# Softmax probabilities of the second attention transposed in ten blocks of 128 columns that cross head limits

## The chip, the cores and the metric

One core of one Trainium2 chip runs the whole program. The metric is the device time of one execution in microseconds (us); the time before is 1310.84 us, the median of three runs (1308.33 to 1314.42).

## The reference, cut to what matters

The program adds four residual blocks to `x` (2 x 1024 tokens x 256): an attention over 154 context tokens, a feed-forward block of eight experts (every token goes through all), a second attention with a mask over the same 154 context tokens, and a routed layer of eight experts. The change touches the second attention alone:

```python
q = xn @ Wq * scale                     # 8 heads of 64
kv = media @ Wkv                        # media: 2 batches x 154 tokens x 256
k, v = jnp.split(kv, 2, axis=-1)
q, k, v = (to_heads(q), to_heads(k), to_heads(v))
sim = jnp.einsum('bhid,bhjd->bhij', q, k)
sim = jnp.where(media_mask[:, None, None, :], sim, neg_inf)
attn = jax.nn.softmax(sim - max(sim), axis=-1)
out = jnp.einsum('bhij,bhjd->bhid', attn, v)
return out.transpose(0, 2, 1, 3).reshape(...) @ Wout
```

## The kernel before

The program has four stages in time: a first attention (0 to about 37 us of the span), the eight dense experts (to about 1046 us), the second attention with the routing of the third layer's tokens woven in (about 1046 to 1262 us), and the routed experts (to the end). Each engine's instruction order is written out by hand, and semaphores join the engines. TensorE (PE) runs its list in order, and so do VectorE (DVE), ScalarE (ACT), GpSimd (POOL) and SyncE (SP, which starts DMAs).

**Preparation of the second attention.** After the last expert product PE computes the keys (L1089) into banks 0 to 3, then the values (L1237): for each of the four halves of 77 context tokens (2 batches x 2 halves, `KH` = 77) two products with 512 moving columns, all heads at once. ACT copies each half into `V1` (L814; the trace calls it V). Then PE transposes the first chunk's normed tokens `xnC2` (L864; it waits for the last value copy and for `c_ln`, the end of DVE's second normalisation of the first chunk, L1327), ACT copies them (`xnT_out`, L749), and PE computes the queries (L1094).

**Chunks and tiles.** There are four chunks of 512 tokens, each of four tiles (j = 0 to 3) of 128 tokens. A tile goes like this:

- PE computes the scores of 8 heads x 154 keys in two halves of four heads (`scores`, L1109 and L1115).
- DVE takes the maxima (`maxes`, L1565), ACT the exponentials into `PC` (`exps`, L763, one instruction per head), DVE the reciprocals of the sums (`dens`, L1573), POOL multiplies by them (`normalise`, L538, a half of 616 columns at a time).
- PE transposes the probabilities (`p_transposes`, L1138). A head's 154 columns are cut in two halves of 77, so there are 16 transposes of 77 columns, in four groups of four. Groups 0 and 2 go to bank 0, which ACT copies to `PTC` (L769); groups 1 and 3 go to bank 1, which DVE copies (L1577). Group 2 waits for the copy of group 0, and group 3 for that of group 1.
- PE multiplies with the values (`attend`, L1148): per head two products, one for each half of 77 keys, 16 in all. Its group g waits for the copy of group g.
- DVE copies the result to `oT` (`o_out`, L1581), PE projects it (`project`, L1157), DVE adds it to the residual (`add_attention`, L1586).

A transpose is one PE record in the trace; an fp32 product is two (so `attend` shows x32). The order on PE in a chunk is: transposes of groups (0, 1) of tile j, `project` of tile j - 1, transposes of groups (2, 3), `attend` of tile j, scores of tile j + 2 or the like. Chunks 1 to 3 weave in the routing of the chunk before (`route`: `logits` L1169, `locations` L1176 to L1179, and on DVE `route_shift`, `route_choice`, `route_places`, `route_slots`; then POOL's `scatter`, L547). Chunks 0 to 2 prepare the next chunk (`front`): DVE's `front_variances`, `front_normed`, `front_variances2`, `front_normed2` (L1314, L1318, L1327, with POOL's power, L468), PE's transposes of `xnC2` and the next queries. After `add_attention` of tile 3 DVE's `route_normed` (L1327, rows) waits until the scatter before it has landed, and the last query copy (`q_out(f, 3)`, L1559) stands behind it.

**In the dense experts** POOL splits the weights (`split_hi`, `split_lo`); in `split_lo` it waits for `down_ps` and then writes `wd_hi` (L511) and `wd_lo` (L513).

## Time and profile before

| | |
|---|---|
| runs | 1308.33, 1310.84, 1314.42 us; median 1310.84 |
| profiled execution | 1310.67 us, of which the span from the first to the last instruction is 1308.9 us |
| busy share of the span | PE 96%, PEld 77%, DVE 70%, ACT 48%, POOL 40% |
| mean granted TensorE clock | 0.983 of full speed |
| second attention, preparation | 1046 to 1067 us |
| chunks 0, 1, 2, 3 from their first transposes of probabilities | 1073.8, 1116.5, 1168.6, 1215.2 us |

All times inside the execution are us from the start of the span. PE is the matrix engine's products, PEld its weight loads, which overlap them. The share of an engine is of busy time; it doesn't say that the others wait for it.

### The profile page before, as it was taken

To read this page: it belongs to the slowest core of one execution; us is meant where nothing else is said; L and a number is where in the kernel's file an instruction comes from. 1 tells how busy PE (TensorE), PEld (TensorE's weight loads), DVE (VectorE), ACT (ScalarE), POOL (GpSimd) and SP (SyncE) were. 2 spreads that over 40 slices of the span, in tenths; PEclk is the share of its full clock that TensorE was granted. 3 is DMA by queue.
4 is the path that set the end of the run, shared out by engine and by line. 5 is a ranking of instruction groups with operands and counts; after the bars stand their busy time and mean duration, and the time that the engine had idled before them with its cause. 6 is when DMAs were issued, how large, how long until landed. Compare 5 with 4: busy or idle time off the path is not lost.

```text
span 1308.9 us, 17566 instructions
## 1 busy us (share of the span) xinstructions
PE 1254.2 (96%) x6162; PEld 1008.3 (77%) x6162; DVE 914.7 (70%) x1643; ACT 624.4 (48%) x1320; POOL 530.1 (40%) x511
## 2 busy tenths in 40 slices
PE   7999999999999999999999999999999989989965
PEld 5778888888888888888888888888888747766754
DVE  5997777767777777777777677777776757757523
ACT  2465544555554555545455454545555343542521
POOL 3654644444444444444444444444442022333314
PEclk9999999999999999999999999999999999989978
DMA  4100500000010000000000001100001210011033
GB/s 132 49 1 1 178 25 25 25 25 25 30 44 25 25 25 25 25 25 25 25 25 26 25 25 41 33 25 25 25 1 49 65 49 17 1 49 49 17 108 128
DMA packets 44392, 50.34 MB, mean 38 GB/s; under 512 B 4289, under 2 KB 40182, under 8 KB 44175
## 3 DMA queue, kind: packets, MB, share of 16 engines
q1 hardware_dynamic: 40144, 43.03, 10.0%
q0 software_dynamic: 2048, 5.55, 1.2%
q8 instruction: 49, 0.80, 0.3%
q10 hardware_dynamic: 2111, 0.63, 0.2%
q14 instruction: 40, 0.33, 0.1%
HBM read 37.35 MB, written 12.62 MB: 38 GB/s over the span
## 4 chain that ended last, share of the span: by engine, by line
PE 87%; DVE 5%; ACT 2%; issue 2%; DMA 2%; POOL 1%; ACTq 0%; SPq 0%; another core or an unknown queue 0%; DVEq 0%; POOLq 0%
PE bank L959 25%; PE bank L958 25%; PE bank L960 25%; PE bank L1138 2%; PE bank L1157 1%; PE bank L1148 1%; ACT PC L763 1%; PE bank L1094 1%; PE bank L1285 1%; DMA slots<-rows,slot_c 1%; PE bank L1115 1%; PE bank L864 1%; DVE nmC L1565 1%; PE bank L1169 1%; PE bank L1237 1%
## 5 line engine op out<-in xcount | busy, mean ns | idle before, releaser
L958 PE MATMUL bank<-xop_hi,w_hi 128*128 128x512 f32 x896 | 350.9, 392 | 1.2 <-ACT half_g L696 1.2
L959 PE MATMUL bank<-xop_lo,w_hi 128*128 128x512 f32 x896 | 351.7, 393 | 0.0
L960 PE MATMUL bank<-xop_hi,w_lo 128*128 128x512 f32 x896 | 350.8, 392 | 0.0
L1505 DVE TENSOR_TENSOR acc<-bank,acc 128x512 f32<-128x512 f32 x248 | 170.8, 689 | 118.7 <-PE bank L960 118.4
L1491 DVE TENSOR_TENSOR hid_lo<-hid,hid_hi 128x512 fp32r<-128x512 f32 x256 | 214.8, 860 | 34.6 <-ACT hid_hi L719 34.5
L958 PE MATMUL bank<-hid_hi,wd_hi 128*128 128x512 f32 x512 | 202.5, 395 | 0.6 <-DVE hid_lo L1491 0.6
L959 PE MATMUL bank<-hid_lo,wd_hi 128*128 128x512 f32 x512 | 203.0, 396 | 0.0
L960 PE MATMUL bank<-hid_hi,wd_lo 128*128 128x512 f32 x512 | 201.4, 393 | 0.0
L958 PEld LDWEIGHTS bank<-xop_hi,w_hi 128*128 128x128 f32 x896 | 168.2, 188 | 42.2 <-ACT half_g L696 1.5
L959 PEld LDWEIGHTS bank<-xop_lo,w_hi 128*128 128x128 f32 x896 | 168.2, 188 | 38.2
L960 PEld LDWEIGHTS bank<-xop_hi,w_lo 128*128 128x128 f32 x896 | 168.1, 188 | 37.4
L704 ACT ACTIVATE s<-bank 128x512 f32<-128x512 f32 x128 | 78.2, 611 | 176.1 <-PE bank L960 176.1
L719 ACT CAST hid_hi<-hid 128x512 fp32r<-128x512 f32 x256 | 157.8, 624 | 1.9 <-DVE hid L1483 1.9
L680 ACT COPY bank<-bank 128x512 f32<-128x512 f32 x128 | 73.0, 570 | 123.7 <-PE bank L960 123.7
L483 POOL TENSOR_TENSOR w_raw<-raw_gu 128x256 f32<-128x256 f32 x32 | 24.1, 752 | 253.2 <-PE bank L960 253.2
L511 POOL CAST wd_hi<-raw_d 128x512 fp32r<-128x512 f32 x32 | 19.5, 611 | 242.3 <-PE bank L960 242.3
L960 PEld LDWEIGHTS bank<-hid_hi,wd_lo 128*128 128x128 f32 x512 | 96.4, 188 | 22.8
L958 PEld LDWEIGHTS bank<-hid_hi,wd_hi 128*128 128x128 f32 x512 | 96.1, 188 | 22.9 <-DVE hid_lo L1491 1.0
L959 PEld LDWEIGHTS bank<-hid_lo,wd_hi 128*128 128x128 f32 x512 | 96.0, 187 | 21.1
L1474 DVE TENSOR_TENSOR hid<-bank,s 128x512 f32<-128x512 f32 x128 | 87.8, 686 | 19.7 <-PE bank L960 19.7
L710 ACT ACTIVATE half_g<-half_g 128x512 f32<-128x512 f32 x128 | 81.2, 634 | 20.7 <-DVE half_g L1464 19.6
L503 POOL TENSOR_TENSOR w_lo<-w_raw,w_hi 128x1024 fp32r<-128x1024 f32 x32 | 86.6, 2707 | 4.0 <-DVE xnA L1327 1.6
(187 smaller groups left out, 1728.7 us busy)
## 6 DMA issues: line engine op xcount, KB each, us to landing
raw_gu<-in_L_ffn_Wg_dram SPq DMA_DIRECT2D x32, 256.0 KB, 2.7
raw_gu<-in_L_ffn_Wu_dram SPq DMA_DIRECT2D x32, 256.0 KB, 3.1
raw_d<-in_L_ffn_Wd_dram SPq DMA_DIRECT2D x32, 256.0 KB, 3.6
slots<-empty_row SPq DMA_DIRECT2D x1, 4112.0 KB, 15.3
kept<-slots SPq DMA_DIRECT2D x8, 258.0 KB, 4.3
x_res<-in_x_dram SPq DMA_DIRECT2D x4, 512.0 KB, 5.2
we_raw<-in_L_ffn_W_dram SPq DMA_DIRECT2D x8, 256.0 KB, 4.6
out_dram<-x_res SPq DMA_DIRECT2D x4, 512.0 KB
```

What stands on the lines that cost most here:

```text
L503: nc.gpsimd.tensor_tensor(out=lo[:, :, W_S1:W_S4 + 1], in0=s[:, :, W_S1:W_S4 + 1], in1=hi[:, :, W_S1:W_S4 + 1].bitcast(F32), op=ALU.subtract)
L680: nc.scalar.copy(bank[FORK_BANK[X]][:], bank[SUM_BANK[X]][:]).then_inc(forked[X], 1)
L704: nc.scalar.activation(out[:], ps[:], ACT.Silu).then_inc(silu_ready[h], 1)
L710: nc.scalar.activation(half["g"][:], half["g"][:], ACT.Silu).then_inc(silu_ready[h], 1)
L719: nc.scalar.copy(hid_hi[n % 2][h][:], hid[h][:]).then_inc(hi_ready[h], 1)
L958: mm(ps, w, a, start=start, stop=False, skip_group_check=True)
L959: mm(ps, w, a_low, start=False, stop=False, skip_group_check=True)
L960: return mm(ps, w_low, a, start=False, stop=True, skip_group_check=True)
L1138: ins = tr(bank[g % 2][0:KH, a * P:(a + 1) * P], PC[j % 2][:, n // 2, n % 2 * KH:(n % 2 + 1) * KH], ident[:])
L1474: nc.vector.tensor_tensor(out=hid[h][:], in0=ps[:], in1=s[:], op=ALU.mult).then_inc(hid_ready[h], 1)
L1491: nc.vector.tensor_tensor(out=hid_lo[n % 2][h][:], in0=hid[h][:], in1=hid_hi[n % 2][h][:].bitcast(F32), op=ALU.subtract).then_inc(lo_ready ...
L1505: nc.vector.tensor_tensor(out=to, in0=ps, in1=to, op=ALU.add).then_inc(acc_added, 1)
```

## The change

Eight heads of 154 columns lie side by side in `PC`, 1232 columns in all. They are now transposed in `PB` = 10 blocks of 128 columns (the last has 80), whatever head the columns belong to, in three groups: blocks 0 to 3 (bank 0, ACT copies 512 columns), 4 to 7 (bank 1, DVE copies 512 columns), 8 and 9 (bank 0, ACT copies 256 columns). Group 0 is issued where groups (0, 1) were, groups 1 and 2 where (2, 3) were. DVE has one copy of `PTC` per tile instead of two.

Seven of the ten blocks hold columns of two heads. `V1` now holds for each batch, block and up to two heads a 128 x 64 slice of the values, with zeros in the rows of the other head, so that `attend` is 17 products with 128 rows (the last block 80). To lay the values out so, ACT makes a copy `ctx2T` of the transposed context with the first 128 tokens appended, PE computes the values block by block (40 products of 128 or 64 moving columns instead of 8 of 512; the last group of the second batch after the transposes of `xnC2`), ACT copies six groups instead of four, and POOL multiplies them by a mask `vmask` (six instructions, `keep_own_heads`, behind the power of the second normalisation). `vmask` is made by 2 memsets and 14 selects on POOL in `split_lo` of the fifth weight quarter (`q == 4`). `attend` of a batch's first tile waits for `c_v`. The wait of the queries for `Wout` moves behind the transposes, and the bias load shares the semaphore `we_in`.

```diff
+    PW = HEADS * KEYS
+    PB = -(-PW // P)
+    P_BLOCKS = (range(0, 4), range(4, 8), range(8, PB))
+    V_BANKS = ((6, 7, 0), (1, 2, 7))
+    C_VALUES = 2 + HB // 2
...
+        PTC = sd.take("PTC", [P, PB, P], F32)
+        ctx2T = sd.take("ctx2T", [P, KB, B, KEYS + P], F32)
+        V1 = sd.take("V1", [P, B, PB, 2, HD], F32)
...
                 if q >= 2:
                     pool.wait_ge(down_ps, 4 * groups_through(q - 2))
+                if q == 4:
+                    v_masks()
                 nc.gpsimd.tensor_copy(wd_hi[i][:], d[:]).then_inc(wd_hi_ready, 1)
...
+            def keep_own_heads(b):
+                for g, of in enumerate(P_BLOCKS):
+                    pool.wait_ge(c_prep_act, C_VALUES + 3 * b + g + 1)
+                    v = V1[:, b, of[0]:of[-1] + 1, :, :].rearrange("p n s d -> p (n s) d")
+                    own = vmask[:, of[0]:of[-1] + 1, :].rearrange("p n s -> p (n s)")
+                    nc.gpsimd.tensor_tensor(out=v, in0=v, in1=own.unsqueeze(2).to_broadcast([P, 2 * len(of), HD]),
+                                            op=ALU.mult).then_inc(c_v, 1)
...
             power(LN_FRONT2, CT, 1)
+            pool.wait_ge(consts_ready, 3)
+            for b in range(B):
+                keep_own_heads(b)
             chunk(0, front=True, route=False)
...
+            act.wait_ge(p4_ps["u"], GROUPS)
+            ctx4 = ctxT[:].rearrange("p k (b n) -> p (k b) n", b=B)
+            wrapped = ctx2T[:].rearrange("p k b n -> p (k b) n")
+            nc.scalar.copy(wrapped[:, :, 0:KEYS], ctx4).then_inc(c_prep_act, 1)
+            nc.scalar.copy(wrapped[:, :, KEYS:KEYS + P], ctx4[:, :, 0:P]).then_inc(c_prep_act, 1)
...
-            for r in range(2 * B):
-                act.wait_ge(c_prep_ps, HB + r + 1)
-                nc.scalar.copy(V1[:, r, :], bank[V_PS[r]][0:KH, :]).then_inc(c_prep_act, 1)
+            for g in range(3):
+                value_out(0, g)
+            for g in range(2):
+                value_out(1, g)
             xnT_out(0)
+            value_out(1, 2)
             q_out(0)
...
             def p_transposes(c, j, groups):
-                pe.wait_ge(c_norm, 2 * t + groups[0] // 2 + 1)
+                pe.wait_ge(c_norm, 2 * t + (1 if groups == (0,) else 2))
+                flat = PC[j % 2][:].rearrange("p h k -> p (h k)")
                 for g in groups:
-                    if g >= 2:
-                        pe.wait_ge(c_pT_act if g % 2 == 0 else c_pT_dve, 2 * t + 1)
-                    for a in range(4):
-                        n = 4 * g + a
-                        ins = tr(bank[g % 2][0:KH, a * P:(a + 1) * P], PC[j % 2][:, n // 2, n % 2 * KH:(n % 2 + 1) * KH], ident[:])
+                    if g == 2:
+                        pe.wait_ge(c_pT_act, 2 * t + 1)
+                    for a, n in enumerate(P_BLOCKS[g]):
+                        w = block_rows(n)
+                        ins = tr(bank[g % 2][0:w, a * P:(a + 1) * P], flat[:, n * P:n * P + w], ident[:])
...
-                for g in range(4):
-                    pe.wait_ge(c_pT_act if g % 2 == 0 else c_pT_dve, 2 * t + 1 + g // 2)
-                    for h in (2 * g, 2 * g + 1):
-                        for k in range(2):
+                if t % (CB * CT) == 0:
+                    pe.wait_ge(c_v, 3 * b + 3)
+                for g, of in enumerate(P_BLOCKS):
+                    if g == 1:
+                        pe.wait_ge(c_pT_dve, t + 1)
+                    else:
+                        pe.wait_ge(c_pT_act, 2 * t + 1 + g // 2)
+                    for n in of:
+                        w = block_rows(n)
+                        for i, h in enumerate(block_heads(n)):
                             ins = mm(bank[5][h % 2 * HD:(h % 2 + 1) * HD, h // 2 * P:(h // 2 + 1) * P],
-                                     V1[:, 2 * b + k, h * HD:(h + 1) * HD], PTC[:, 2 * h + k, :], start=k == 0, stop=k == 1)
+                                     V1[0:w, b, n, i, :], PTC[0:w, n, :], start=n == head_blocks(h)[0], stop=n == head_blocks(h)[-1])
...
+            def values(b, g):
+                for a, n in enumerate(P_BLOCKS[g]):
+                    first, heads = n * P % KEYS, block_heads(n)
+                    cols = slice(INNER + heads[0] * HD, INNER + (heads[-1] + 1) * HD)
+                    for k in range(KB):
+                        ins = mm(bank[V_BANKS[b][g]][:, a * P:a * P + len(heads) * HD], ctx2T[:, k, b, first:first + P],
+                                 Wkvs[:, k, cols], start=k == 0, stop=k == KB - 1)
                 ins.then_inc(c_prep_ps, 1)
...
+            values(0, 0)
+            values(0, 1)
+            pe.wait_ge(c_prep_act, 3)
+            values(0, 2)
+            pe.wait_ge(c_prep_dve, 1)
+            values(1, 0)
+            pe.wait_ge(c_prep_act, 4)
+            values(1, 1)
+            pe.wait_ge(c_prep_act, C_VALUES + 4)
             pe.wait_ge(c_ln, 1)
             transpose_chunk(xnC2, (0, 1), 0, c_xnT_ps)
+            values(1, 2)
             pe.wait_ge(c_xnT, 2)
+            pe.wait_ge(c_prep_dve, HB // 2)
+            pe.wait_ge(wout_in, 16)
             queries(0)
...
                 maxes(c, 1, 1)
+                dens(c, 1, 0)
                 pT_out(c, 0, 1)
-                dens(c, 1, 0)
-                pT_out(c, 0, 3)
                 dens(c, 1, 1)
...
-                pT_out(c, 1, 1)
                 dens(c, 2, 0)
                 add_attention(c, 0)
-                pT_out(c, 1, 3)
+                pT_out(c, 1, 1)
...
-                pT_out(c, 3, 1)
                 if with_front:
                     front_variances2(f)
                 add_attention(c, 2)
-                pT_out(c, 3, 3)
+                pT_out(c, 3, 1)
```

## Rows read from the trace of the kernel before

**Rows 1.** Page: the chain that ended last, share of the span by engine.
```profile
PE 87%; DVE 5%; ACT 2%; issue 2%; DMA 2%; POOL 1%; ACTq 0%; SPq 0%; another core or an unknown queue 0%; DVEq 0%; POOLq 0%
```
**Rows 2.** Busy time by stretch: PE, PEld, DVE, ACT, POOL, then granted clock, DMA.
```profile
1067.00:1102.70 35.70, 32.68 (x321) 27.10 (x322) 26.26 (x70) 17.71 (x74) 11.84 (x10) 1.00 0.01 1
...
1160.00:1168.50 8.50, 7.68 (x46) 6.00 (x46) 4.35 (x13) 5.08 (x22) 2.43 (x2) 0.63 0.00 0
...
1237.00:1251.50 14.50, 13.54 (x105) 12.00 (x105) 7.41 (x22) 1.62 (x3) 6.08 (x6) 0.76 0.17 64
```
**Rows 3.** Instructions of L1138 and L1148: ns min/median/max, first and last start.
```profile
L1138 PE MATMUL bank<-ident,PC x256: 272/273/497, 1073.8 to 1246.3; 128*77 128x128 f32 x128
L1148 PE MATMUL bank<-PTC,V x512: 272/273/454, 1076.2 to 1248.3; 77*64 77x128 f32 x171
```
**Rows 4.** Timeline of chunk 0, tile 0: start, us, engine, instruction, idle before.
```profile
1073.77 1.10 PE L1138 MATMUL bank<-ident,PC 128*77 128x128 f32 x8 [0.62 <-DVE x_res L1538]
...
1074.47 0.58 ACT L769 COPY PTC<-bank 77x512 f32<-77x512 f32 x1
...
1075.19 1.12 PE L1138 MATMUL bank<-ident,PC 128*77 128x128 f32 x8 [0.33 <-ACT PTC L769]
...
1076.24 2.02 PE L1148 MATMUL bank<-PTC,V 77*64 77x128 f32 x32
```
**Rows 5.** Timeline of chunk 2, from tile 2 to the next queries.
```profile
1187.69 0.58 ACT L769 COPY PTC<-bank 77x512 f32<-77x512 f32 x1
...
1188.42 1.07 PE L1138 MATMUL bank<-ident,PC 128*77 128x128 f32 x8 [0.95 <-ACT PTC L769]
...
1190.45 2.02 PE L1148 MATMUL bank<-PTC,V 77*64 77x128 f32 x32
...
1194.15 1.39 DVE L1314 BATCH_NORM_STATS2 stats<-xnC 128x6 f32<-128x256 f32 x4
...
1197.28 1.38 DVE L1327 TENSOR_SCALAR xnC<-xnC,mv,rstd 128x256 f32<-128x256 f32 x4
...
1201.38 7.03 PE L1094 MATMUL bank<-xnTc,Wqs 128*128 128x512 f32 x16
```
**Rows 6.** Timeline of the preparation: values, second normalisation, first queries.
```profile
1049.97 7.03 PE L1237 MATMUL bank<-Wkvs,ctxT 128*77 128x512 f32 x16
...
1055.05 1.02 POOL L468 TENSOR_TENSOR rstd<-ve,mhalf 128x4 f32<-128x4 f32 x1 [3.56 <-DVE ve L1321]
...
1056.10 1.38 DVE L1327 TENSOR_SCALAR xnC<-xnC,mv,rstd 128x256 f32<-128x256 f32 x4 [0.75 <-POOL rstd L468]
...
1057.67 1.09 PE L864 MATMUL bank<-ident,xnC 128*128 128x128 f32 x8 [0.67 <-ACT V L814]
...
1059.86 7.13 PE L1094 MATMUL bank<-xnTc,Wqs 128*128 128x512 f32 x16 [1.10 <-ACT xnTc L749]
```
**Rows 7.** Timeline of DVE and POOL side by side, in chunk 0.
```profile
1092.04 2.30 DVE L1327 TENSOR_SCALAR xnC<-x_res,mv,rstd 128x256 f32<-128x256 f32 x4
1092.20 1.34 POOL L538 TENSOR_TENSOR PC<-PC,rdenC 128x616 f32<-128x616 f32 x1 [1.39 <-DVE rdenC L1573]
```
**Rows 8.** Timeline of the dense experts: DVE beside POOL, and (1020 us) without it.
```profile
136.72 2.96 DVE L1483 TENSOR_TENSOR hid<-half_u,half_g 128x512 f32<-128x512 f32 x2
...
137.37 1.76 POOL L505 TENSOR_TENSOR w_lo<-raw_gu,w_hi 128x512 fp32r<-128x512 f32 x1
...
1020.25 1.28 DVE L1483 TENSOR_TENSOR hid<-half_u,half_g 128x512 f32<-128x512 f32 x2
```
**Rows 9.** Instructions of L459: ns min/median/max.
```profile
L459 POOL TENSOR_SCALAR_AFFINE_SELECT ident<-ident x1: 292/292/292, 2.8 to 2.8; 128x128 f32<-128x128 f32 x1
```
**Rows 10.** Page, groups: busy us, mean ns, idle before and its releaser.
```profile
L511 POOL CAST wd_hi<-raw_d 128x512 fp32r<-128x512 f32 x32 | 19.5, 611 | 242.3 <-PE bank L960 242.3
```
**Rows 11.** Waits from 1067 to 1262 us: total, times, longest.
```profile
DVE rows L1327 <- DMA slots<-rows,slot_c: 6.9, 2, 4.3
```
**Rows 12.** Waits before 1050 us, from 1000 us on: total, times, longest.
```profile
ACT k1T L810 <- PE bank L1089: 10.3, 2, 8.6
```

More of the change, by code:

```diff
@@ L180, in flamingo_kernel @@
         token_id = keep.take("token_id", [P, NT], U32)
+        vmask = keep.take("vmask", [P, PB, 2], F32)
         empty_row = keep.take("empty_row", [P, ROW], F32)
@@ L254, in flamingo_kernel @@
         be_all = sg.take("be_all", [P, E, D], F32)
-        V1 = sg.take("V1", [KH, 2 * B, INNER], F32)
         rows = sg.take("rows", [P, CT, ROW], F32)
@@ L263, in flamingo_kernel @@
         PC = [sd.take(f"PC{i}", [P, HEADS, KEYS], F32) for i in range(2)]
-        PTC = sd.take("PTC", [KH, 2 * HEADS, P], F32)
+        PTC = sd.take("PTC", [P, PB, P], F32)
+        ctx2T = sd.take("ctx2T", [P, KB, B, KEYS + P], F32)
+        V1 = sd.take("V1", [P, B, PB, 2, HD], F32)
         nmC = [sd.take(f"nmC{i}", [P, HEADS], F32) for i in range(2)]
@@ L767, in pT_out @@
             def pT_out(c, j, g):
-                act.wait_ge(c_pT_ps, 4 * (c * CT + j) + g + 1)
-                nc.scalar.copy(PTC[:, 4 * g:4 * g + 4, :].rearrange("p a b -> p (a b)"), bank[0][0:KH, :]).then_inc(c_pT_act, 1)
+                act.wait_ge(c_pT_ps, 3 * (c * CT + j) + g + 1)
+                of = P_BLOCKS[g]
+                nc.scalar.copy(PTC[:, of[0]:of[-1] + 1, :].rearrange("p a b -> p (a b)"),
+                               bank[0][:, 0:len(of) * P]).then_inc(c_pT_act, 1)
             def xn4T_out(r, banks=ROUTE_T, of=range(CT), part=0):
@@ L1214, in chunk @@
                 attend(c, 2)
-                p_transposes(c, 3, (0, 1))
+                p_transposes(c, 3, (0,))
                 if route:
@@ L1231, in _ @@
             pe.wait_ge(acc_added, 4 * GROUPS)
-            for r in range(2 * B):
-                if r == 2:
-                    pe.wait_ge(c_prep_act, 1)
-                    pe.wait_ge(c_prep_dve, 1)
-                for k in range(KB):
-                    ins = mm(bank[V_PS[r]][0:KH, :], ctxT[:, k, r * KH:(r + 1) * KH], Wkvs[:, k, INNER:2 * INNER],
-                             start=k == 0, stop=k == KB - 1)
-                ins.then_inc(c_prep_ps, 1)
-            pe.wait_ge(c_prep_act, 2 * B + HB // 2)
+            pe.wait_ge(c_prep_act, 2)
+            def values(b, g):
[5 more added lines that the diff above has]
+                                 Wkvs[:, k, cols], start=k == 0, stop=k == KB - 1)
+                ins.then_inc(c_prep_ps, 1)
+            values(0, 0)
[7 more added lines that the diff above has]
+            pe.wait_ge(c_prep_act, C_VALUES + 4)
+            pe.wait_ge(c_ln, 1)
+            transpose_chunk(xnC2, (0, 1), 0, c_xnT_ps)
+            values(1, 2)
+            pe.wait_ge(c_xnT, 2)
             pe.wait_ge(c_prep_dve, HB // 2)
             pe.wait_ge(wout_in, 16)
-            pe.wait_ge(c_ln, 1)
-            transpose_chunk(xnC2, (0, 1), 0, c_xnT_ps)
-            pe.wait_ge(c_xnT, 2)
             queries(0)
+            pe.wait_ge(c_prep_act, C_VALUES + 3 * B)
             scores_after_queries(0)
```

57 lines of the change are left out of this document (40 added, 17 removed).

## The prediction

> **What bounds the kernel now.** I read the chain that ended last first: PE carries 87% of it [rows 1]. Most of that is the dense experts, which the change leaves alone, so I went on to the second attention, by stretch [rows 2]. There PE is busy 32.7 of 35.7 us in chunk 0: it sets the pace, with short waits. The granted clock is 1.00 there, but 0.63 from 1160 to 1168.5 us and 0.76 from 1237 to 1251.5 us. The timeline of single tiles then shows where PE waits: in chunk 0 for ACT's copy of group 0 (0.33 us) [rows 4], in chunk 2, tile 2 for the same copy (0.95 us) [rows 5]. Last I read the preparation, where the first queries wait for `xnTc`, hence for the transposes at 1057.67, and those start 0.19 us after DVE's second normalisation (1056.10 + 1.38 = 1057.48), released by the last value copy: a near tie of two chains [rows 6]. So the change has a profit side, four chunks, and a cost side, 20 us of preparation, and each has to be priced by what ends last there.
>
> **The transposes.** One record lasts 0.27 us [rows 3], eight in a row 1.10 us [rows 4]: a spacing of (1.10 - 0.27) / 7 = 0.118 us. Would a block of 128 columns cost more than one of 77? The eight transposes of `xnC2` have 128 columns and take 1.09 us [rows 6], so no. Six fewer per tile save 6 x 0.118 = 0.71 us.
>
> **The products.** `attend` shows 32 records in 2.02 us [rows 4]: (2.02 - 0.27) / 31 = 0.056 us each, 0.113 us for a product. The seventeenth adds 0.11 us. That 128 rows stream as fast as 77 is not shown by any row with 64 columns of weights; I take it so, since L1138 (77 columns) and L864 (128) differ in nothing and the shape that matters here, 64 columns, stays. The other end is 0.118 us a record (the transposes' spacing), see the rivals. PE's sum is 0.71 - 0.11 = 0.60 us a tile, 9.6 us in 16 tiles: the upper end of the profit.
>
> **What of it reaches the end.** I shifted the timeline.
>
> - Tile 0 of a chunk starts with a wait of DVE or ACT. The second group of transposes now starts without waiting, and only blocks 8 and 9 wait for ACT's copy, which comes as before at 1074.47 + 0.58 = 1075.05. PE waited until 1075.19, then made eight; now two: `attend` starts 0.7 to 0.8 us earlier and ends 0.7 us earlier [rows 4].
> - Tile 1 is PE's own order: plus 0.6 us, 1.3 in all. In chunk 1 to 3 DVE's `route_choice` follows ACT's `route_exp`, which stands behind the last copy of tile 1, so it moves by the same 1.3 us.
> - Tile 2 in chunks 1 to 3: PE's 0.95 us of waiting was for a copy that ends at 1187.69 + 0.58 = 1188.27, behind the exponentials of tile 3, hence behind `route_choice` [rows 5]. It moves by 1.3 us. Four of the transposes after it are group 1 now and lie in the wait, so two are left of eight: plus 0.7, less 0.1 for the product: 1.9 us.
> - Tile 3: PE could give 0.6 more, but DVE's two normalisations stand between (1194.15 and 1197.28 to 1198.66) [rows 5]. The copy of group 1 that stood ahead of `front_variances2` goes, so DVE gains too. By the moved list the end of `front_normed2` gains 2.3, the queries 2.2 us.
>
> So 2.2 us for chunks 1 and 2. Chunk 0 has no such wait for ACT in tile 2, and `front_normed` with POOL beside it takes 2.3 us: 1.7 us. Chunk 3 ends with the routing chain on DVE, behind its last tiles: 2.0 us. Sum: 1.7 + 2.2 + 2.2 + 2.0 = 8.1 us. Behind chunks 1 and 2 `route_normed` waits for the scatter (6.9 us in two waits) [rows 11]; its start, `slot_c`, stands behind `o_out` of tile 3 and moves with it, so the gain passes. Lower end 6 us: DVE's single copy now stands behind `dens` and `add_attention`; by my list it ends about 0.1 us before `attend` needs group 1 in tiles 1 and 3, and if it is 0.3 us late in seven such tiles, 2.1 us go.
>
> **The ACT and DVE copies.** DVE loses one copy a tile and ACT 256 columns of one; both lie beside PE but for the places named. Nothing more is counted.
>
> **The masks.** At most 14 selects of 0.29 us (the row is for 128 columns, these have one) [rows 9] and two memsets, some 4.5 us, once, ahead of `wd_hi`. POOL idles 242.3 us in 32 times before that line [rows 10], 7.6 us each, waiting for PE; PE needs the result more than an iteration later. Zero; without this cover 4.5 us. ACT's two context copies (616 and 512 columns, by L769 about 0.7 and 0.6 us) fall into the 8.6 us that ACT idles before the first key copy [rows 12]: zero, else 1.3 us.
>
> **The values.** Before: 16 records from 1049.97, 7.03 us [rows 6]. After: of the 80 records 72 lie ahead of the transposes of `xnC2` (18 blocks x 2 halves of the contraction x 2). Each loads 128 columns of weights and streams 128 or 64; the nearest row is L864, 0.117 us: 72 x 0.117 = 8.4 us, so PE is free at 1049.97 + 8.4 = 1058.4, and the transposes start there instead of at 1057.67. The other eight records lie in the 1.1 us in which PE waits for `xnTc` [rows 6]. Alone: +0.7 us.
>
> **POOL against DVE.** This is the larger cost. POOL's six mask multiplications start when the power at 1055.05 + 1.02 = 1056.07 is done, the same moment that releases DVE's four instructions at 1056.10 [rows 6]. In chunk 0 one POOL product of 1.34 us beside the same four instructions makes them 2.30 us instead of 1.38: +0.92 [rows 7]. Do several in a row cost several times as much? In the dense experts two DVE products that take 1.28 us alone took 2.96 us beside two POOL operations in sequence: DVE gets in between them, one for one [rows 8]. The mask operations of 512 columns are 1.34 x 512 / 616 = 1.1 us, those of 256 0.6 us [rows 7]. With three between DVE's four: 1.1 + 1.1 + 0.6 = 2.8 us, with a fourth ahead 3.9. `c_ln` then comes at 1057.48 + 2.8 to 3.9 = 1060.3 to 1061.4, behind PE's 1058.4. Ends for the whole preparation: +0.7 us (PE alone) and +3.9 us. I take 2.7 us, the case of three, since the transposes stood 0.19 us behind `c_ln`.
>
> The page SBUF — State Buffer of the Trainium skill (section "Who interferes with whom") says that GpSimd and a VectorE operation that takes the shared ports exclude each other for the whole instruction. The stretch of two alternating operations agrees. By that rule alone, taken as four full blocks, the time would be 1.2 us above mine; by the row with one block, 1.8 us below.
>
> The page TensorE: Matmul & The Clock Gate (section "Part 2: What happens when you issue a matmul") prices a weight load by its columns, 128 / 1.2 = 107 ns, and says rows don't matter. By it the 72 records are an estimated 7.7 us, and the products with 128 rows cost what they cost with 77; no run here shows the latter.
>
> **Sum.** The profiled execution is 1310.67 us, 0.17 below the median. 1310.67 - 8.1 + 2.7 = 1305.3 us. A change of 0.5% (6.6 us) is about what a measurement tells from none.
>
> **The rivals.**
>
> - *Cheap preparation.* DVE gets through ahead of POOL's masks, or waits for one only: 1310.67 - 8.1 + 0.7 = 1303.3 us. If besides a clock drop goes away, less: the stretch from 1237 us, at 0.76, loses up to 0.24 x 14.5 = 3.5 us by it [rows 2], so 1299.8 us. For it: the tie at 1056.1. Against: POOL has five of the six operations ready by then. Chance 0.34.
> - *The single DVE copy is late.* The profit sinks to 5 us or less, the preparation costs 2.7: 1308.4 us. For it: margins of 0.1 us. Against: what now stands ahead of it is short, and DVE has one copy less. Or PE, idle from 1058.4 to 1060.3, is granted half the clock in the first queries, as it is from 1160 us on; as much as there, (1 - 0.63) x 8.5 = 3.1 us [rows 2], gives 1308.4 us. Chance of either 0.20.
> - *Slower: the products of 128 rows stream at the transposes' pace.* 34 records x (0.118 - 0.056) = 2.1 us a tile, 34 us in 16: 1339 us. It decides for slower from 12 us over 544 records, 0.022 us a record, on. For it: every row at 0.056 us has at most 77 rows. Chance 0.04.
> - *The change does not shorten the tiles*, since DVE or ACT are the real pace: 1310.67 + 2.7 = 1313.4 us. Against: PE's busy share of 92% in chunk 0 [rows 2]. Chance 0.04.
>
> **The numbers.** Forecast 1305.3 us with chance 0.38; its own range, 1303.9 to 1307.6, comes from 2.8 to 3.9 us for the masks and 7.0 to 9.6 us of profit. For 8 in 10: from the cheap preparation with one clock drop fewer, 1299.8, to the late copy with a clock drop more, 1311. Faster by over 0.5% means below 1304.3: the cheap preparation and a tenth of the forecast's case, 0.38. Slower by over 0.5%: the last two in part and an unlucky clock, 0.08. Between them 0.54.
>
> **What would show it.** L1138 with 160 records, `attend` with 34 in about 2.1 us; the transposes of `xnC2` at 1060 instead of 1057.67, L1327 before them 3.9 us long beside POOL; `attend` of chunk 2, tile 2 starting 20 us after the chunk's first transposes instead of 21.9; no wait of PE for `PTC` by DVE. Wrong it would be if `attend` stretches beyond 2.2 us, if L1327 stays at 1.4 to 2.3 us, or if the clock drops at other places than before.

## The result and the profile after

The changed kernel takes 1303.17 us (median of 18 runs, 1299.66 to 1310.85) against 1311.49 us for the kernel before (18 runs, 1308.33 to 1317.40). The ratio is 0.9936, 95% interval 0.9922 to 0.9949: 0.64% faster. The forecast was 1305.3 us. The time lies in the range for 8 in 10, 1299.8 to 1311 us, but below the forecast's own range of 1303.9 to 1307.6 us, and on the "faster" side of the 0.5% line, where the larger chance had been given to "between them". The profiled execution took 1299.66 us, span 1297.8 us. It is the lowest of the 18, with a mean granted clock of 0.987 against 0.983 in the profile before, so the 11.1 us between the two spans hold more than the change; they have to be read by stretch. In the line numbers of the kernel after, L1199 is the transposes (L1138 before), L1215 `attend` (L1148), L1154 the queries (L1094), L924 the transposes of `xnC2` (L864) and L1407 DVE's normalisation (L1327).

Instructions of the transposes and of `attend` in the kernel after, with duration in ns (minimum, median, maximum); they answer to [rows 3]:

```profile
L1199 PE MATMUL bank<-ident,PC x160: 272/273/332, 1078.9 to 1235.0; 128*128 128x128 f32 x144, 128*80 128x128 f32 x16
L1215 PE MATMUL bank<-PTC,V x544: 270/273/325, 1080.6 to 1237.1; 128*64 128x128 f32 x171, 80*64 80x128 f32 x11
```

Timeline after, chunk 0, tile 0 (answers to [rows 4]):

```profile
1078.90 1.09 PE L1199 MATMUL bank<-ident,PC 128*128 128x128 f32 x8 [0.62 <-DVE x_res L1618]
1079.60 0.59 ACT L814 COPY PTC<-bank 128x512 f32<-128x512 f32 x1
1080.04 0.69 DVE L1658 COPY PTC<-bank 128x512 f32<-128x512 f32 x1
1080.24 0.44 PE L1199 MATMUL bank<-ident,PC 128*128 128x128 f32 x2 [0.24 <-ACT PTC L814]
1080.60 2.24 PE L1215 MATMUL bank<-PTC,V 128*64 128x128 f32 x34
```

Both groups of four now run in one block, only two transposes stand behind ACT's copy, and `attend` starts 1.70 us after the first transpose instead of 2.47. It lasts 2.24 us where [rows 4] have 2.02: 0.22 us more for one product (two records).

Timeline after, chunk 2, tile 2 and the next queries (answers to [rows 5]):

```profile
1182.36 0.60 PE L1199 MATMUL bank<-ident,PC 128*128 128x128 f32 x4
1182.76 0.60 ACT L814 COPY PTC<-bank 128x512 f32<-128x512 f32 x1
1183.40 0.44 PE L1199 MATMUL bank<-ident,PC 128*128 128x128 f32 x2 [0.44 <-ACT PTC L814]
1184.81 2.24 PE L1215 MATMUL bank<-PTC,V 128*64 128x128 f32 x34
...
1195.42 4.88 PE L1154 MATMUL bank<-xnTc,Wqs 128*128 128x512 f32 x11
```

The chunk's first transposes are at 1165.06. `attend` of tile 2 starts 19.75 us later (21.88 before), the queries 30.36 us later (32.81 before). PE still waits for ACT's copy, but only for what the four transposes of group 1 leave of it: 0.44 us instead of 0.95.

Timeline after, preparation (answers to [rows 6]):

```profile
1052.70 8.20 PE L1306 MATMUL bank<-Wkvs,ctx2T 128*128 128x64 f32 x72
1057.78 1.02 POOL L485 TENSOR_TENSOR rstd<-ve,mhalf 128x4 f32<-128x4 f32 x1 [3.55 <-DVE ve L1401]
1058.75 4.82 POOL L554 TENSOR_TENSOR V<-V,vmask 128x512 f32<-128x512 f32 x5
1058.83 3.84 DVE L1407 TENSOR_SCALAR xnC<-xnC,mv,rstd 128x256 f32<-128x256 f32 x4 [0.76 <-POOL rstd L485]
1062.82 1.06 PE L924 MATMUL bank<-ident,xnC 128*128 128x128 f32 x8 [1.91 <-DVE xnC L1407]
1064.98 1.55 PE L1154 MATMUL bank<-xnTc,Wqs 128*128 128x512 f32 x3 [0.26 <-ACT xnTc L793]
```

PE is through with its 72 records at 1060.90 and waits 1.91 us for DVE, whose four instructions take 3.84 us instead of 1.38 beside POOL's masks. This profile runs 2.73 us behind the one before from the dense experts on, because of a stretch at half clock there. Windows of the kernel after (columns: PE, PEld, DVE, ACT, POOL busy, granted clock, DMA share, GB/s); the last two answer to [rows 2]:

```profile
62.00:69.00 7.00, 7.00 (x19) 5.49 (x18) 6.89 (x17) 3.27 (x6) 1.17 (x1) 0.51 0.24 80
...
1160.00:1168.50 8.50, 7.77 (x87) 6.47 (x85) 5.93 (x18) 8.29 (x37) 4.02 (x4) 1.00 0.01 2
1237.00:1251.50 14.50, 9.51 (x59) 8.45 (x55) 7.17 (x34) 3.06 (x7) 1.56 (x3) 0.83 0.15 51
```

The two spans by stretch, in us, each read off the timelines of the two profiles:

| stretch | before | after | difference |
|---|---|---|---|
| start to the first key product | 1045.82 | 1048.55 | +2.73 |
| first key product to first queries | 14.04 | 16.43 | +2.39 |
| chunks 0, 1, 2: first transposes to next queries | 28.92, 32.81, 32.81 | 26.96, 30.37, 30.36 | -6.85 |
| queries to first transposes, chunk 2 | 19.27 | 15.02 | -4.25 |
| chunk 3: first transposes to the start of the last projection | 34.33 | 29.62 | -4.71 |
| the rest | 100.9 | 100.5 | -0.4 |

Two rows hold a stretch at half clock in the kernel before alone, behind the queries of chunk 2 (1159.5 to 1166.3 us) and from `attend` of tile 2 of chunk 3 on (1238.0 to 1244.8 us). In chunk 3, `attend` of tile 2 starts 2.07 us earlier (20.43 us after the chunk's first transposes instead of 22.50), and most of the rest of the 4.71 us lies in the slowed records after it. What belongs to the change is +2.39 - 6.85 - 2.07 = -6.5 us; the medians differ by 8.3 us (6.7 to 10.2 by the interval). Both kernels have one profile each for this sum.

### The profile page after: what moved, and what is told of

Its sections match the earlier page's. It is cut to its first block, busy times and chain, and to the rows that moved or that the text cites. A ratio compares the mean times of both kernels' runs of the same rounds, so it can differ in the third digit from the quotient of the medians.

```text
span 1297.8 us, 17571 instructions
## 1 busy us (share of the span) xinstructions
PE 1245.1 (96%) x6162; PEld 1003.2 (77%) x6162; DVE 908.3 (70%) x1627; ACT 623.4 (48%) x1324; POOL 538.1 (41%) x533
## 4 chain that ended last, share of the span: by engine, by line
PE 86%; DVE 5%; ACT 3%; issue 2%; DMA 1%; POOL 1%; another core or an unknown queue 0%; ACTq 0%; SPq 0%; DVEq 0%; POOLq 0%
PE bank L1019 25%; PE bank L1018 25%; PE bank L1020 25%; PE bank L1215 2%; ACT PC L807 2%; PE bank L1224 1%; PE bank L1154 1%; PE bank L1199 1%; PE bank L1365 1%; DVE nmC L1645 1%; DMA slots<-rows,slot_c 1%; PE bank L1175 1%; PE bank L1236 1%; POOL slots L588 1%; DVE xnC L1407 0%
```

## The experiments

**1. POOL's products alone, in the old layout.** Six products of the masks' sizes on tiles of their own, behind the same power, and nothing else of the change; six memsets of these tiles stand ahead.

```diff
+            for t in extra:
+                ins = nc.gpsimd.memset(t[:], 1.0)
...
             power(LN_FRONT2, CT, 1)
...
+            for t in extra:
+                nc.gpsimd.tensor_tensor(out=t[:], in0=t[:], in1=ones[...], op=ALU.mult)
```

> The kernel before with six POOL products of the masks' shapes (four of 512, two of 256 columns, on tiles of their own) behind the power of the second normalisation, nothing else. Theory (POOL blocks DVE there): DVE's four instructions take about 3.8 us instead of 1.38, the transposes of xnC2 start 2.3 us later behind the last value copy or later still, the queries too: 10.0 to 10.2 us from the first value record to the transposes instead of 7.70. Rival: they stay at 7.7 us, since the values or their copies set that time.

One run took 1318.07 us. Timeline of this kernel, preparation:

```profile
1051.33 2.42 POOL L572 MEMSET extra<- 128x512 f32 x6
1051.41 3.46 DVE L1335 TENSOR_SCALAR xnC<-x_res,mv,rstd 128x256 f32<-128x256 f32 x4 [0.81 <-POOL rstd L469]
...
1057.98 5.39 POOL L577 TENSOR_TENSOR extra<-extra,ones 128x512 f32<-128x512 f32 x6
1058.06 3.84 DVE L1335 TENSOR_SCALAR xnC<-xnC,mv,rstd 128x256 f32<-128x256 f32 x4 [0.76 <-POOL rstd L469]
1062.05 1.94 PE L872 MATMUL bank<-ident,xnC 128*128 128x128 f32 x8 [5.17 <-DVE xnC L1335]
```

DVE takes 3.84 us, to the hundredth what it takes in the changed kernel: the lengthening is POOL's alone. From the first value product to the transposes it is 12.2 us, not the 10.0 to 10.2 us expected, because the memsets lengthen the first normalisation as well (3.46 us instead of 1.38). They do it in another way than the products. Durations in ns (minimum, median, maximum) of DVE's four instructions beside the memsets, and of those beside the masks in the changed kernel:

```profile
L1335 DVE TENSOR_SCALAR xnC<-x_res,mv,rstd x4: 395/402/2494, 1051.4 to 1054.5; 128x256 f32<-128x256 f32 x4
L1407 DVE TENSOR_SCALAR xnC<-xnC,mv,rstd x4: 699/1126/1127, 1058.8 to 1061.5; 128x256 f32<-128x256 f32 x4
```

All six memsets pass beside one DVE instruction, which takes 2.49 us; the other three take the usual 0.40 us. The POOL products take turns with DVE: the first starts 0.08 us ahead of DVE's first, and three more lie between DVE's four, whose durations are 1.12, 1.13, 0.70 and 1.13 us instead of 0.41. So four products stand ahead of DVE's last instruction, but each of 512 columns costs 0.72 us and the one of 256 columns 0.29 us, about 0.33 us less than POOL needs for it (1.05 to 1.10 and 0.66 us); 0.33 us is what lies between the starts of two of DVE's instructions when POOL is quiet.

The first queries come 19.15 us after the first key product instead of 14.04, of which the memsets' share on DVE is 2.08 us and the products' 2.46. The clock was cut, too: it fell to half at 1060.4 us, with PE idle since 1056.9 us, and rose again at 1070.6 us. The changed kernel with its 1.91 us of idleness doesn't show that here. Windows of this kernel:

```profile
1057.00:1062.00 5.00, 0.00 (x0) 0.00 (x0) 4.14 (x5) 0.50 (x1) 5.00 (x6) 0.84 0.00 0
1062.00:1072.00 10.00, 9.09 (x18) 4.63 (x19) 0.57 (x1) 2.15 (x3) 1.37 (x2) 0.57 0.00 0
```

The chunks 1 and 2, at full clock, take 32.80 and 32.79 us here, as in the profile before, so the stretches of the old order can be read again from run to run.

**2. The masks behind the normalisation.**

```diff
             pool.wait_ge(consts_ready, 3)
+            pool.wait_ge(c_ln, 1)
             for b in range(B):
                 keep_own_heads(b)
```

> The changed kernel with POOL's six mask products held back until the second normalisation of the first chunk is done (c_ln). Theory (POOL's products block DVE's four instructions one for one, which took 3.84 us instead of 1.38): they take 1.4 us again, the transposes of xnC2 then wait for PE's 72 value records and start about 8.4 us after the first of them instead of 10.1 us, and the first queries start 1.7 us earlier than in the changed kernel; median 1301.5 us. Rival (the preparation is set by PE and ACT, the long DVE instructions are a coincidence of the same wait): the queries start where they did, median 1303.2 us. A second rival: the masks, now later, delay the first normalisation of probabilities and the gain is given back in tile 0.

1298.49 us (6 runs), ratio to the kernel before 0.9910 (0.9882 to 0.9938), where 1301.5 us was expected. Timeline:

```profile
1059.19 1.38 DVE L1408 TENSOR_SCALAR xnC<-xnC,mv,rstd 128x256 f32<-128x256 f32 x4 [0.76 <-POOL rstd L485]
...
1060.70 5.19 POOL L554 TENSOR_TENSOR V<-V,vmask 128x512 f32<-128x512 f32 x6 [1.55 <-issue]
1061.10 1.04 PE L925 MATMUL bank<-ident,xnC 128*128 128x128 f32 x8
...
1063.29 7.13 PE L1155 MATMUL bank<-xnTc,Wqs 128*128 128x512 f32 x16 [0.31 <-ACT xnTc L794]
```

DVE is back at 1.38 us, PE doesn't wait, and the queries come 14.37 us after the first key product: 2.06 us of the 2.39 are gone, and 0.33 us are what PE's own 72 records cost. The masks hold nobody up: they end at 1065.9, and the first transposes of probabilities ahead of `attend` are at 1077.2.

But little of the 2.06 us is left behind chunk 0. In this profile the clock is at half from 1076.7 to 1083.5 us, in the chunk's first tile, and chunk 0 takes 29.51 us instead of 26.96. From the first key product to the queries behind chunk 0 it is 57.80 us, against 57.31 in the changed kernel's profile and 58.32 in its control's (experiment 5), which has 3.4 us at half clock there. The two other kernels with late masks (experiment 6) have the same 6.8 us at half clock. So the wait is shown to pay in the preparation, and not shown to pay behind it.

Nor can the median be set beside the changed kernel's 1303.17 us. This kernel ran side by side with those of experiments 1 and 4 and the one with sixteen transposes of experiment 3. In all four profiles the stretch from the start of the last projection to the end takes 56.2 to 56.4 us, the old layout among them, and in the ten others 58.2 to 59.8 us; the cause isn't known. The kernel of experiment 4, which doesn't have the wait, got nearly the same ratio beside it, 0.9913.

**3. Is it PE's records, or the new grouping?** Two kernels from either side: the kernel before with six of its sixteen transposes of a tile left out (three each of groups 1 and 3, so part of `PTC` is stale), and the changed kernel with groups 0 and 2 transposed twice, sixteen in all.

```diff
-                    for a in range(4):
+                    for a in range(4 if g % 2 == 0 else 1):
```

> The kernel before, with six of its sixteen transposes of each tile left out (three each of groups 1 and 3, so part of PTC is stale), and all copies, waits and products as before. It asks whether PE's records alone make the profit. Theory (PE sets the pace; 6 x 0.118 = 0.71 us a tile): from first transposes to the next queries chunk 1 and 2 take 32.81 - 2.8 = 30.0 us, or more where the waits for ACT's and DVE's copies of groups 0 and 1 now come to light. Rival (the new grouping and the copy that DVE no longer makes carry a good part of it): 31.4 us or more.

```diff
-                    for a, n in enumerate(P_BLOCKS[g]):
+                    for a, n in list(enumerate(P_BLOCKS[g])) * (1 if g == 1 else 2):
```

> The changed kernel with ten transposes raised to sixteen: groups 0 and 2 are made twice, into the same place (eight in the first call, eight in the second, as before the change). Copies, products and DVE's work stay. Theory (the six transposes fewer on PE are what paid): of the 2.0 us that chunk 0 and the 2.45 us that chunks 1 and 2 got shorter from their first transposes to the next queries, at least 1.8 and 2.0 us come back (28.8 us and 32.4 us); median about 1311 us. Rival (the DVE copy less is what paid): the chunks stay at 27.0 and 30.4 us, median 1303 us.

The old kernel with ten transposes took 1310.9 us in its one run, the new one with sixteen 1305.57 us (12 runs), ratio to the kernel before 0.9967 (0.9948 to 0.9987). Chunk 1 of four profiles, from the chunk's first transpose to the start of `attend` of each tile and to the next queries, us, all at full clock:

| | tile 0 | tile 1 | tile 2 | tile 3 | queries |
|---|---|---|---|---|---|
| before | 2.47 | 11.98 | 21.89 | 27.61 | 32.81 |
| old order, ten transposes | 2.10 | 11.28 | 20.85 | 26.25 | 31.45 |
| new order, sixteen | 2.36 | 12.08 | 21.06 | 26.96 | 31.82 |
| after | 1.70 | 10.77 | 19.76 | 25.51 | 30.37 |

Fewer transposes in the old order give 1.36 us of the 2.44, and the new order with all sixteen gives 0.99: together 2.35, nearly the whole. The 0.99 us are the order less the dearer `attend` of seventeen products, with DVE's one copy less in them, too. My theories that the records alone carry it both fell: ten transposes should have brought 2.8 us, and sixteen should have taken back at least 2.0 us (32.4 us, a median of 1311 us), where 1.45 came back. The rival's 31.4 us for the old order was met; the rival that DVE's copy alone pays (30.4 us) was not. The timeline of the old order with ten, tile 2 of chunk 1, shows why: PE wins time ahead and loses it again at the copy, whose time ACT's exponentials set.

```profile
1138.09 0.77 PE L1138 MATMUL bank<-ident,PC 128*77 128x128 f32 x5
1139.14 1.99 PE L1157 MATMUL bank<-Wouts,oT 128*128 128x256 f32 x8 [0.28 <-DVE oT L1581]
1142.09 0.74 PE L1138 MATMUL bank<-ident,PC 128*77 128x128 f32 x5 [0.95 <-ACT PTC L769]
```

The 0.95 us are as long as those of [rows 5]. What shortens them is the order of the groups: in the new one, four transposes that were behind the copy lie ahead of it.

**4. DVE's second copy put back as filler.** Three `bn_stats` of 128 columns (0.67 us) where DVE's first copy of a tile stood.

```diff
+            def as_long_as_a_copy():
+                for i in range(3):
+                    nc.vector.bn_stats(idle_stats[:, i, :], before[:, 0:P])
```

> The changed kernel with some 0.7 us of idle work on DVE in each tile (three bn_stats of 128 columns), where the copy of group 1 stood before. Theory (PE sets the pace, DVE's copy less paid only in tile 3, ahead of the two normalisations): chunks grow by 0.7 us at most each, from 27.0 and 30.4 us to 27.7 and 31.1 us; median 1303 to 1306 us. Rival (DVE's copy less is what paid): all comes back, 28.9 and 32.8 us, median 1311 us.

1298.82 us (5 runs), ratio 0.9913 (0.9882 to 0.9945): no loss. Chunks 0, 1 and 2 take 27.19, 30.73 and 30.59 us, 0.23 to 0.36 more than after; the rival's 28.9 and 32.8 us didn't come. Of the 0.36 us of chunk 1, 0.15 us are a delay ahead of tile 3 that the control has without a filler (25.66 us instead of 25.51). So the copy that DVE no longer makes gives a tenth of the profit of a chunk, or little more, as far as a filler stands for it: it takes the time of the copy and doesn't wait for PE as the copy did. (The median lies below the 1303 to 1306 us expected. These five runs had a median clock of 0.987, those of the changed kernel 0.984, and the profile has the short end told of in experiment 2, so the 4 us between the medians aren't the filler's.)

**5. Why does the seventeenth product cost 0.22 us?** Inside `attend`, behind the first ten records, records start 52 to 57 ns apart in both kernels (the first ten come in pairs, mostly 13 and 96 ns apart), but in the changed one the starts of records 16 to 18 are 109 ns apart, where head 4 has three products in a row. First the control, the changed kernel itself beside what follows:

> The changed kernel itself, as a control beside the three that follow. Expected: ratio 0.992 to 0.995 to the kernel before. If on this chip it comes out near 0.990, the masks behind the normalisation bought nothing in the median and the 1298.5 us measured for them was the chip.

1304.97 us (7 runs), ratio 0.9940 (0.9914 to 0.9966). Then block 6 with its heads turned:

```diff
-                        for i, h in enumerate(block_heads(n)):
+                        for i, h in list(enumerate(block_heads(n)))[::-1 if n == 6 else 1]:
```

> Only the order of two products is changed: in block 6 head 5's product comes ahead of head 4's, so that head 4 no longer has three products in a row in the same 64 columns of the PE array. Theory A (what stretches attend from 1.745 to 1.968 us between its first and last start is the third product in a row in the same half): the starts at 109 ns between records 16 and 18 go back to 52 to 57 ns, first to last start becomes about 33 x 0.0555 = 1.83 to 1.86 us, each of the 16 tiles gets up to 0.11 us shorter, 1.8 us in all, most of it in the chunks' tiles 1 and 3. Rival B (the slow place is where the record's weights have rows of zeros or where the group of products changes its semaphore): 109 ns gaps stay at records 16 to 18 whatever the order, and nothing is gained.

1303.85 us (10 runs), ratio 0.9935 (0.9916 to 0.9954). The slow place moved to records 24 to 26, and nothing was gained; neither A nor B had foretold that. The rows of `attend` in chunk 1 follow for four kernels, each with what PE does next, in tile 3 but for one. Block 6 turned:

```profile
1146.42 2.24 PE L1215 MATMUL bank<-PTC,V 128*64 128x128 f32 x34
1148.59 0.66 PE L924 MATMUL bank<-ident,xnC 128*128 128x128 f32 x4
```

An eighteenth product, once in the upper half (head 5's first one made twice) and once in the lower (head 4's):

```diff
-                        for i, h in enumerate(block_heads(n)):
+                        for i, h, twice in [(i, h, False) for i, h in enumerate(block_heads(n))][:1] + [(1, 5, True)] * (n == 6) + [(i, h, False) for i, h in enumerate(block_heads(n))][1:]:
...
-                                     V1[0:w, b, n, i, :], PTC[0:w, n, :], start=n == head_blocks(h)[0], stop=n == head_blocks(h)[-1])
+                                     V1[0:w, b, n, i, :], PTC[0:w, n, :], start=n == head_blocks(h)[0], stop=twice or n == head_blocks(h)[-1])
```

(the lower one with `[(1, 4, True)] * (n == 4)`).

> The changed kernel with an eighteenth product a tile: head 5's first product is made twice (it overwrites the same values). Turning block 6 moved the slow place from records 16 to 18 to records 24 to 26 and left the sum of the starts at 1.968 us, so the third product in a row is not the cause. New theory C: the two halves of 64 columns (even heads write partitions 0 to 63, odd ones 64 to 127) work side by side, each at 0.109 us a record, and the fuller half sets the time: 16 records of each before give 16 x 0.109 = 1.744 us (measured 1.745), 18 lower and 16 upper now 18 x 0.109 = 1.962 us (measured 1.968). This product goes to the upper half, which then has 18 as well: free, first to last start within 1.96 to 2.02 us with 36 records. Rival D (every record costs the same and something else makes one gap): about 1.968 + 0.11 = 2.08 us.

> The changed kernel with head 4's first product made twice: 20 records in the lower half, 16 in the upper. Theory C: 20 x 0.109 = 2.18 us from first to last start. Rival D: 2.08 us, the same as with the upper product.

The eighteenth product in the upper half:

```profile
1145.92 2.46 PE L1215 MATMUL bank<-PTC,V 128*64 128x128 f32 x36
1148.31 0.77 PE L924 MATMUL bank<-ident,xnC 128*128 128x128 f32 x5
```

In the lower half (tile 2 of its chunk):

```profile
1143.38 2.46 PE L1215 MATMUL bank<-PTC,V 128*64 128x128 f32 x36
1145.77 0.44 PE L1199 MATMUL bank<-ident,PC 128*128 128x128 f32 x2
```

Both take 0.22 us more again, 2.187 us from first to last start. Theory C met the lower product and failed on the upper one, which it had free; D's 2.08 us was missed by both. One run each gave 1305.29 and 1310.34 us beside 1316.75 of the kernel before. Last, the order low, high, low, high:

```diff
+                low = [(h, n) for h in range(0, HEADS, 2) for n in head_blocks(h)]
+                high = [(h, n) for h in range(1, HEADS, 2) for n in head_blocks(h)]
...
+                for h, n in [p for pair in zip(low, high) for p in pair] + low[len(high):]:
```

> The changed kernel with the seventeen products of attend ordered low, high, low, high (even heads write partitions 0 to 63, odd ones 64 to 127), the odd one last. Theory C fell: eighteen products take 2.187 us whichever half gets the extra one. New theory E: two neighbours in the list run side by side only if they are of different halves, each product in one pair at most, 0.218 us for a pair or for a single. Order low low high high ... gives 1 + 7 pairs + 1 = 9 slots before (1.745 us), 10 slots with three low ones in a row or with block 6 turned (both 1.968), 11 with either eighteenth product (both 2.187). Alternating gives 8 pairs and 1 single, 9 slots: 1.745 to 1.76 us from first to last start, 0.22 us a tile less, up to 3.5 us in 16 tiles; at most two thirds of that reaches the chunks if it goes as with the transposes, so 2 to 3.5 us. Rival F (each product beyond sixteen costs 0.22 us in any order): stays at 1.968 us and nothing is gained.

```profile
1145.79 2.18 PE L1219 MATMUL bank<-PTC,V 128*64 128x128 f32 x34
1147.90 0.87 PE L924 MATMUL bank<-ident,xnC 128*128 128x128 f32 x6
```

1307.43 us (9 runs), ratio 0.9951 (0.9926 to 0.9977). `attend` is 0.06 us shorter, chunks 1 and 2 are 0.1 us shorter (30.26 and 30.25), and the starts now come in pairs 7 and 102 ns apart, but for the last product: its first record starts 98 ns after the one before, its second 110 ns after the first. Theory E fell: it had 1.76 us from first to last start where 1.91 came out. F's 1.968 is nearer, but wasn't met either: in this order the seventeenth product costs 0.16 us, not 0.22. One reading fits the changed kernel and three of the four variants (the alternating order to 0.06 us): two products of different halves share 0.218 us, and whoever has no partner takes 0.218 us alone. 16 products are 8 pairs, 17 are 8 pairs and a single. The kernel with the eighteenth upper product doesn't fit: that product should have been the single's partner and wasn't. Its slow places are records 16 to 18 and the last two, so the two unpaired products stand far apart; whether the distance is the reason isn't settled, and the same product in an even order wasn't tried.

**6. The masks late, with each order of the products.**

```diff
+            pool.wait_ge(c_ln, 1)
```

> Block 6 turned, and POOL's masks behind the second normalisation. If the two costs add up (2.06 us of the preparation, up to 1.8 us of the tiles): 3 to 3.9 us below the control, about 1299.5 us where the control has 1303. If the preparation's gain is only passed on to a clock drop in the first queries or first tiles, 1 to 2 us below the control.

> Alternating halves and POOL's masks behind the second normalisation together. Theory: 2.1 us of the preparation and 2 to 3.5 us of the tiles less than the changed kernel: ratio to the kernel before 0.989 to 0.990. If clock drops take back what PE saves, 0.991 as the masks alone.

| same chip | masks at once | masks behind the normalisation |
|---|---|---|
| block 6 turned | 0.9935 (0.9916 to 0.9954), 1303.85 us | 0.9908 (0.9880 to 0.9936), 1301.89 us |
| halves alternate | 0.9951 (0.9926 to 0.9977), 1307.43 us | 0.9917 (0.9892 to 0.9942), 1301.86 us |

By the ratios the one wait gives 3.5 and 4.5 us, by the medians 2.0 and 5.6 us, and in each row the two intervals overlap. The first kernel is 3.1 us below the control, as far as expected if the costs add up, but no gain of the turned block is in that. The second, at 0.9917, misses the 0.989 to 0.990 of its theory and meets the case in which clock drops take back what PE saves.

The profiles show that case. With the masks late, both kernels have their first queries 14.37 us after the first key product (16.43 with the masks at once), and both are at half clock for 6.8 us in the first tile of chunk 0, where the same orders with the masks at once have 3.4 us. Windows of that tile: block 6 turned, masks at once, then masks late; halves alternating, masks at once, then masks late:

```profile
1076.00:1084.00 8.00, 6.92 (x64) 5.56 (x62) 5.98 (x21) 5.09 (x25) 4.81 (x4) 0.79 0.00 0
...
1076.00:1084.00 8.00, 7.37 (x56) 6.20 (x54) 5.10 (x18) 3.94 (x18) 4.63 (x4) 0.57 0.00 0
...
1076.00:1084.00 8.00, 6.92 (x66) 5.44 (x66) 5.71 (x21) 4.79 (x24) 4.51 (x4) 0.79 0.00 0
...
1076.00:1084.00 8.00, 7.38 (x56) 6.16 (x56) 5.14 (x18) 3.93 (x18) 4.35 (x4) 0.57 0.00 0
```

From the first key product to the queries behind chunk 0 the wait leaves 0.66 us of its 2.06 in the first pair (58.49 to 57.83) and 0.63 in the second (58.21 to 57.58). What else the ratios gain isn't assigned. The order of the products gives nothing that these runs can tell. The three kernels with the late masks have the lowest ratios, 0.991 to 0.992, but the filler kernel has 0.9913 without them; a gain of the late masks in the whole time is likely, and not shown beyond doubt.

## Why the prediction was right, and where it was off

**Transposes.** Right in kind: 160 records of 273 ns, with 128 columns at the pace of 77. The 0.118 us is a mean, though: the first gap in a row of eight is 0.17 us and the others 0.109 us, in both kernels, so six fewer save 0.65 us and not 0.71.

**Products.** The step "the seventeenth adds 0.11 us" was mis-sized: it adds 0.22 us [rows 4 beside the row of L1215]. By the reading of experiment 5, a mean over 32 records prices a product that shares its time with another, and the odd one has no partner. The prediction's own sign of being wrong, `attend` beyond 2.2 us, came true with 2.24 us. PE's sum is 0.65 - 0.22 = 0.43 us a tile, 6.9 us in 16, not 9.6. The four chunks gained more than that, 8.9 us: PE's sum isn't the upper end that the prediction took it for, because the new order takes waits away as well. The rival of products at the transposes' pace fell: the records with 128 rows keep the 52 to 57 ns of those with 77. The page TensorE: Matmul & The Clock Gate of the Trainium skill (section "Part 3: Packing small matmuls — row/col tiling") says that products in different column groups run concurrently. The starts at half the transposes' spacing agree, and so do those 7 ns apart in the alternating order.

**What of it reaches the end.** Forecast 1.7, 2.2 and 2.2 us for chunks 0 to 2, measured 1.96, 2.44 and 2.45; for chunk 3, 2.0 against 2.07. By tiles, chunk 1 gained 0.77, 1.21, 2.13, 2.10 and, at the queries, 2.44 us (forecast 0.7, 1.3, 1.9, then 2.2). The hand-moved list was right in its place, tile 2, and the reason, and 0.2 us a chunk short, though it had the product too cheap. The copy that tile 2 waits for moved by 1.42 us, not 1.3: it starts 19.12 us after the first transposes of chunk 2 before and 17.70 us after. The mechanism there, that the order and not the count brings a good part, was in the list, but my own expectation in experiment 3 had forgotten it. DVE's single copy was never late: the instructions of L1199 and L1215 show no wait of PE for it, and the filler shows room.

**Masks and context copies at zero.** Right in the number. The two memsets and fourteen selects, twelve of 0.18 us and two of 0.6 to 0.7 us, don't lie inside POOL's wait for PE but right behind its end, from 175.71 to 178.8 us. They push that iteration's `wd_hi` back by 3.0 us and shorten POOL's next wait (6.15 us instead of 8.74). PE is busy 30.00 of the 30.00 us from 170 to 200 us in both kernels:

```profile
L543 POOL TENSOR_SCALAR_AFFINE_SELECT vmask<-vmask x7: 180/184/187, 175.9 to 178.5; 128x1 f32<-128x1 f32 x7
L545 POOL TENSOR_SCALAR_AFFINE_SELECT vmask<-vmask x7: 182/185/704, 176.1 to 178.6; 128x1 f32<-128x1 f32 x7
```

The 2.73 us lost ahead of the keys are the half clock from 62.2 us, before the masks exist; the old kernel with ten transposes has it as well, at 61.8 us, and reaches the keys at 1048.53.

**Preparation.** Forecast 2.7 us (PE alone 0.7), measured 2.39 (PE alone 0.33; the 72 records took 8.20 us where 8.4 was forecast). The number is near by luck, two errors against each other. The products that stand ahead of DVE's last instruction are four, one ahead and three between, which was the case priced at 3.9 us and not the one taken; but each costs 0.72 or 0.29 us, not its whole 1.1 or 0.6. Together they add 2.46 us. The 3.9 us written as the length of L1327 was the sum for four products; by the prediction's own working DVE's four would have taken 1.38 + 2.8 = 4.2 us, so that the measured 3.84 is near 3.9 doesn't confirm it. The "cheap preparation" fell, although its 1303.3 us is nearest to the median: right time, wrong reason. On the page SBUF — State Buffer of the Trainium skill (section "Who interferes with whom") the shared ports belong to one of the two for a whole instruction. The trace agrees: DVE's four instructions end 0.15 or 0.16 us after POOL's first four, each in its turn. The memsets of experiment 1 block DVE too, in one piece of six.

**The sum.** The profiles put the change at -6.5 us where the forecast had -5.4: 0.3 us of the difference come from the preparation, 0.8 from the chunks. The medians have 8.3. The difference of 1.8 us isn't assigned. One part could be the scatter ahead of chunk 2: from its first issue to DVE's next `rows` it took 9.24 us before and 7.61 after, but 8.1 in the old kernel with ten transposes. The two profiles of the old order with sixteen have 9.2 and 9.0 us, the eleven of the new order 7.6 to 8.3 us: some of it may belong to the change, and it varies by itself. The rows that answer to [rows 11] and [rows 12]:

```profile
DVE rows L1407 <- DMA slots<-rows,slot_c: 5.6, 3, 2.9
```

```profile
ACT k1T L868 <- PE bank L1149: 9.1, 2, 7.5
```

The other is the clock: the runs of the changed kernel spread over 11 us with mean clocks from 0.976 to 0.987, about 0.9 us for 0.001. The stretches at half clock came at other places than before, which was the third of the prediction's signs of being wrong; what they cost was not in its sum. In seven of the eleven profiles of the changed order one lies in chunk 0 (the control from 1078.2 us on, 0.79 from 1078 to 1086 us). The runs don't say whether the change makes them rarer.

## What to carry to other kernels

Price a saving at the wait that ends it: here the fewer instructions gave 1.4 us of 2.4 a chunk, and moving independent ones ahead of the copy that PE waits for gave the other 1.0, with a dearer `attend` paid from it. A new POOL instruction is to be placed by what DVE does in the same microseconds, not by when its input is ready: one wait that holds it back by some 2 us bought 2.06 us of the preparation in three profiles. Then follow the gain to the next stages: a longer stretch at half clock took 1.4 us of it back in both pairs that can be compared. A mean per instruction over a row is not the price of one more: it had the transpose 8% too dear and the odd product at half its cost.

## What the runs showed of the hardware that was not expected

- Products with 64 columns of weights, in the two halves of 64 columns in turn: 0.109 us each for 16; the seventeenth 0.22, the eighteenth 0.22 in either half; with the halves in strict alternation the seventeenth 0.16.
- DVE's four normalisations of 256 columns take 1.38 us alone, 3.46 beside six POOL memsets (one of the four takes 2.49) and 3.84 beside POOL products (each of the four is lengthened), the latter in two kernels alike.
- In the preparation with PE idle for 5.17 us the granted clock fell to half within the idleness, at 1060.4 us, and stayed there to 1070.6 us; with 1.91 us idle it stayed at 1.00 in the first queries.
- The scatter of four DMAs ahead of chunk 2, to DVE's next `rows`, took 7.6 to 9.2 us with the same data.
